# Working out the token places of two batches at the head of an attention's fourth round

## The reference

```python
logits = xf @ gate_w + gate_b
probs = jax.nn.softmax(logits, axis=1)
topk_p, topk_i = jax.lax.top_k(probs, TOP_K)
...
rank = jnp.cumsum(mask.astype(jnp.int32), axis=0)
slot = jnp.where(mask & (rank <= C), rank - 1, C)
...
xin = x_pad[idx]
h = jax.nn.relu(jnp.einsum('ecd,edh->ech', xin, w1) + b1[:, None, :])
out = jnp.einsum('ech,ehd->ecd', h, w2) + b2[:, None, :]
```

## Time and profile before

| | |
|---|---|
| Median of 3 runs | 1766.37 us (1758.09 to 1767.57) |
| The profiled execution | 1775.01 us, its span 1773.3 us |
| TensorE busy | 1382.5 us (78%) |
| VectorE busy | 1011.9 us (57%) |
| ScalarE busy | 690.0 us (39%) |
| GpSimd busy | 461.2 us (26%) |
| Mean granted TensorE clock | 0.868 of full speed |

### The profile page before, as it was taken

One profiled execution on the slowest core, in us unless ns is written; L12 is line 12 of the kernel. 1 busy time (PEld: TensorE's weight loads), 2 busy tenths in 40 slices (PEclk: granted clock), 3 DMA queues, 4 the chain that ended last, 5 costly groups with the idle time before them and its releaser, 6 DMA issues. The chain is left out here.

```text
span 1773.3 us, 26739 instructions
## 1 busy us (share of the span) xinstructions
PE 1382.5 (78%) x9650; PEld 837.1 (47%) x9650; DVE 1011.9 (57%) x2471; ACT 690.0 (39%) x1868; POOL 461.2 (26%) x577
## 2 busy tenths in 40 slices
PE   3677845858989948675886798989978967887998
PEld 2333423635555625353332456565655543344665
DVE  6554551154556643166454667676675864555886
ACT  3233431246656514242334455555542133333121
POOL 1000042244423342342000385858450001000000
PEclk8577867979999978787898799899898978988999
DMA  2443011150000010211000000000000010000000
GB/s 49 127 124 99 11 43 55 38 108 10 4 1 1 1 59 30 85 56 33 8 2 1 1 1 1 1 1 1 1 1 1 1 23 8 9 2 1 7 6 13
DMA packets 66999, 45.40 MB, mean 26 GB/s; under 512 B 17564, under 2 KB 60261, under 8 KB 66869
## 3 DMA queue, kind: packets, MB, share of 16 engines
q1 hardware_dynamic: 61013, 34.48, 7.3%
q0 software_dynamic: 4096, 8.40, 1.8%
q10 hardware_dynamic: 1760, 0.82, 0.2%
HBM read 24.91 MB, written 13.89 MB: 22 GB/s over the span
## 5 line engine op out<-in xcount | busy, mean ns | idle before, releaser
L3191 ACT ACTIVATE L2a_pr<-psum,L2a_negmax 128x512 f32<-128x512 f32 (+3 forms) x256 | 131.9, 526 | 131.8 <-DVE L2a_negmax L3261 73.3
L550 ACT ACTIVATE L1x_praw<-psum,L1x_negmax 128x154 f32<-128x154 f32 x256 | 96.2, 391 | 78.7 <-DVE L1x_negmax L642 78.5
L3059 PE MATMUL psum<-ident,L2a_pr 128*128 128x128 f32 x640 | 96.6, 301 | 34.1 <-DVE L2a_pT L3281 20.0
L312 POOL TENSOR_TENSOR L1x_pm<-L1x_praw,L1x_total 128x1024 f32<-128x1024 f32 x32 | 60.8, 1899 | 159.4 <-DVE L1x_total L648 102.4
L3059 PEld LDWEIGHTS psum<-ident,L2a_pr 128*128 128x128 f32 x640 | 81.1, 156 | 41.3 <-issue 25.1
L1519 DVE TENSOR_REDUCE L0x_negmax<-psum 128x6 f32<-128x924 f32 (+1 forms) x48 | 47.7, 1011 | 79.3 <-PE psum L1065 76.3
L1519 DVE TENSOR_REDUCE L3x_negmax<-psum 128x6 f32<-128x924 f32 (+1 forms) x48 | 47.8, 1011 | 69.2 <-PE psum L1065 58.1
L1519 DVE TENSOR_REDUCE L2x_negmax<-psum 128x6 f32<-128x924 f32 (+1 forms) x48 | 47.8, 1011 | 60.0 <-PE psum L1065 53.0
L642 DVE TENSOR_REDUCE L1x_negmax<-psum 128x4 f32<-128x616 f32 x64 | 50.8, 795 | 54.4 <-PE psum L364 50.6
L1957 DVE SCALAR_TENSOR_TENSOR L3f_acc<-psum,L3f_comb,L3f_acc 128x128 f32<-128x128 f32 x256 | 72.0, 343 | 8.4 <-PE psum L1861 5.0
L2950 POOL TENSOR_TENSOR L2a_pr<-L2a_pr,L2a_total 128x1024 f32<-128x1024 f32 x32 | 60.7, 1896 | 51.4 <-DVE L2a_total L3289 51.4
(11 more groups left out here) (695 smaller groups left out, 3548.3 us busy)
## 6 DMA issues: line engine op xcount, KB each, us to landing
expert_arena<-in_L_ffn_w SPq DMA_DIRECT2D x16, 256.0 KB, 4.9
group_in<-zero SPq DMA_DIRECT2D x2, 1472.0 KB, 11.2
L1f_xs<-group_in SPq DMA_DIRECT2D x10, 256.0 KB, 4.1
group_out<-L1f_ys SPq DMA_DIRECT2D x10, 256.0 KB, 2.6
...
```

What stands on the lines that cost most here:

```text
L312: nc.gpsimd.tensor_tensor(pm[:, n % 2].rearrange("p j t k -> p (j t) k"), praw[:, n % 3, :, :, 0:MAIN].rearrange("p j t k -> p (j t) k"), ...
L550: nc.scalar.activation(praw[:, n % 3, j, t, :], psum[:, 2 * u + j, x * CTX:(x + 1) * CTX], ACT.Exp, bias=negmax[:, n % 2, u, j, x:x + 1], ...
L3059: last = nc.tensor.transpose(psum[:, TURN + n // 4, n % 4 * P:(n % 4 + 1) * P], pr[:, m % RING, n * P:(n + 1) * P], core.ident[:])
L3191: ins = nc.scalar.activation(pr[:, i % RING, SEQ * j + lo:SEQ * j + hi], psum[:, bank + j, lo:hi], ACT.Exp, bias=negmax[:, i % RING, e:e + ...
```

## The change

In the fourth round (b = 3) the steps of group 0 move to its head: `rowsT` of both batches and `logits` ahead of the second chunk's scores, `best` ahead of `normalised(2)` on VectorE, `ranks` ahead of `output(2)`. Their variance root and `front` move into the third round. `HOSTED` goes from 5 to 6, which is 12 scatters in place of 10, and each pair after the first waits until the pairs before it have landed. `best` of group 1 moves from `sparse_experts` to the end of the attention; its one-hot choices get a tile of their own, `oh1`. In `sparse_experts` the `ranks` of group 1 go ahead of group 2's transposes.

```diff
@@ TensorE, round b
                     scoresT(b, 0)
+                    if dispatch and b == B - 1:
+                        pe.wait_ge(s["mx"], UNITS * B)
+                        pe.wait_ge(s["added"], B - 2)
+                        dispatch.rowsT(pe, 0, 0, xns[0], 1)
...
                     products(b - 1, NG)
+                    if dispatch and b == B - 1:
+                        pe.wait_ge(dispatch.s["xt"], 1)
+                        dispatch.rowsT(pe, 0, 1, xns[1], 1)
                     scores(f, 0, 1)
                     sums(b - 1, NG)
+                    if dispatch and b == B - 1:
+                        pe.wait_ge(s["mrow"], 2 * B)
+                        dispatch.logits(pe, 0, turned, 0)
...
-                    if dispatch and b == B - 1:
-                        pe.wait_ge(s["mrow"], 2 * B)
-                        dispatch.rowsT(pe, 0, 0, xns[0], 0)
...
                     if dispatch and b == B - 1:
-                        pe.wait_ge(s["added"], B - 2)
-                        dispatch.rowsT(pe, 0, 1, xns[1], 1)
+                        pe.wait_ge(dispatch.s["lg"], 1)
+                        dispatch.ranks(pe, 0, 0)
                     output(b - 1)
                     scoresT(b, 2)
-                    if dispatch and b == B - 1:
-                        dispatch.logits(pe, 0, turned, 0)
...
-                    if dispatch and b == B - 1:
-                        pe.wait_ge(dispatch.s["lg"], 1)
-                        dispatch.ranks(pe, 0, 0)
                     scoresT(b, 4)
@@ ScalarE, round b
                     exps(b, 0)
+                    if dispatch and b == B - 1:
+                        dispatch.rows_out(act, 0, turned[0], 1)
...
+                    if dispatch and b == B - 1:
+                        dispatch.rows_out(act, 1, turned[1], 1)
                     values(b - 1)
                     exps(b, 1)
-                    if dispatch and b == B - 1:
-                        for x in range(2):
-                            dispatch.rows_out(act, x, turned[x], x)
...
                     exps(b, 3)
+                    if dispatch and b == B - 2:
+                        dispatch.spread_root(act, 0)
                     if f < B:
                         max_rows(2 * f)
                     exps(b, 4)
...
-                    if dispatch and b == B - 2:
-                        dispatch.spread_root(act, 0)
@@ VectorE, round b
                     maxima(f, 0, 2)
-                    if dispatch and b == B - 1:
-                        dve.wait_ge(s["xt_ps"], B)
-                        dispatch.front(dve, v, 0, first_rows)
...
+                    if dispatch and b == B - 1:
+                        dispatch.logits_in(dve, 0, tmp["lg"], 0)
+                        dispatch.best(dve, v, 0, tmp["lg"], tmp)
                     normalised(b - 1)
+                    if dispatch and b == B - 1:
+                        dispatch.place(dve, v, 0, tmp, 0)
...
                     if dispatch and b == B - 1:
-                        dispatch.logits_in(dve, 0, tmp["lg"], 0)
-                        dispatch.best(dve, v, 0, tmp["lg"], tmp)
                         dispatch.front(dve, v, 1, dispatch.rows)
-                        dispatch.place(dve, v, 0, tmp, 0)
...
                     maxima(f, 6, 7)
+                    if dispatch and b == B - 2:
+                        dve.wait_ge(s["xt_ps"], B)
+                        dispatch.front(dve, v, 0, first_rows)
                     maxima(f, 7, 8)
...
                 kept(B - 1)
+                if dispatch:
+                    dispatch.best(dve, v, 1, dispatch.lg1[:], middle)
@@ Dispatch
-    HOSTED = 5
+    HOSTED = 6
@@ Dispatch.scatter
         for n in range(first + t0, first + t1):
+            if k == 0 and t0 == 0 and n:
+                pool.wait_ge(self.s["spread"], 16 * 2 * n)
             for r in range(2):
@@ sparse_experts, TensorE
+                dispatch.ranks(pe, 1, RANK)
                 dispatch.rowsT(pe, 2, 3, xn, 3)
                 dispatch.logits(pe, 2, [xnT], LOGITS)
-                dispatch.ranks(pe, 1, RANK)
@@ sparse_experts, VectorE
                 dispatch.front(dve, v, 2, xn)
-                dispatch.best(dve, v, 1, dispatch.lg1[:], tmp[1])
                 dispatch.place(dve, v, 1, tmp[1], RANK)
```

4 lines of the change are left out of this document (added).

## The result

The changed kernel takes 1779.32 us (median of 6, 1767.50 to 1784.32), the kernel before, run beside it, 1760.40 (6 runs, 1758.09 to 1767.57). The ratio of their runs is 1.0089, 95% interval 1.0062 to 1.0116: 15.7 us slower, with 10.9 to 20.4 in the interval (the medians lie 18.9 apart). The forecast was 1773 with 1763 to 1781, and "same" with 0.70. The time lies in the range. The change is slower by more than 0.5%, to which the forecast gave 0.27.

A forecast was written before the change was run, and what follows sets the result against it. GpSimd's chain of sixteen scatters before the read of slots_in was taken as the bound. Its first expert-stage scatter 9.1 + 3.6 = 12.7 us late, less 6.3 gained, gives +6.4: 1773 us from 1766.4, range 1763 to 1781.

The forecast's parts named there:

- P: First GpSimd scatter of the expert stage, after the barrier; forecast 12.7 us late, 9.1 without the lower clock.
- What the change gives behind the seam: Expert stage: the chain of sixteen scatters starts 5.2 us after P instead of 11.5, so 6.3 us sooner.
- Third round's end … Net +1.4: Moved root and its table load +1.5, eight row operations +1.2, exponential's table load saved −1.3: net +1.4 us.
- Fourth round's head: Transposes, logits and VectorE's choice come ahead of batch 2's normalising: its reciprocal at 223.3, 8.5 us late.
- Rival 4: Change is faster: VectorE has a gap for the choice and the output product isn't held; −3.5 us, 1763, chance 0.10.
- The clock in the fourth round, +3.6: TensorE's wait before batch 2's output product brings half clock for some 10 us; four slower groups, +3.6 us.
- Rival 1: TensorE's clock holds through the fourth round: +2.8 us, 1769, chance 0.22.
- rival 2: TensorE's clock stays low to the fourth round's end: +11 us, 1777, chance 0.20.
- From batch 3's reciprocal to P: 9.0 us to VectorE's drain, 3.4 for batch 2's choice, 1.76 from drain to first expert-stage scatter.
- GpSimd beside it: Paced hosted scatters, 4.3 us a pair (3.5 to 5.6): GpSimd's drain at 256.6, about together with VectorE's.
- rival 3: Paced scatters on GpSimd end last at the barrier, at 5.6 us a pair: +10 us, 1776, chance 0.06.
- Downstream only the start moves: Behind the read of slots_in everything shifts in start only; no term added to the sum.

The follow-up runs named there:

- choice_six: Kernel before with batch 2's choice at the attention's end, its rank products first in the expert stage, twelve unpaced hosted scatters: 1760.38 us, ratio 1.0016.
- before_again: The kernel before, unchanged, run once more for a second profile: 1760.61 us, ratio 1.0009.
- delay2: Kernel before plus four unused tiles cleared and a drain on GpSimd ahead of batch 3's scatters in the expert stage: 1780.76 us, ratio 1.0093 to the kernel before.
- fill3: Changed kernel plus eight needless identity products on TensorE ahead of the third round's scores that wait for the maxima: 1763.94 us, ratio 1.0026 to the kernel before.
- root_behind: Changed kernel with the variance root behind the third round's copy of the maxima instead of ahead: 1763.12 us, ratio 1.0013 to the kernel before.
- norm_first: Changed kernel with batch 2's normalising ahead of logits and choice on VectorE, ranks behind the second chunk's sums on TensorE: 1789.89 us, ratio 1.0050 to the kernel before.
- fill4: Changed kernel plus sixteen needless identity products on TensorE between the ranks and batch 2's output product: 1780.95 us, ratio 1.0085 to the kernel before.
- six_paced: Kernel before with batch 2's choice at the attention's end, its ranks first in the expert stage, twelve hosted scatters paced in pairs: 1770.11 us, ratio 1.0045.
- unpaced: Changed kernel without the waits between pairs of hosted scatters: 1797.85 us, ratio 1.0104 to the kernel before.

## Why the prediction was right or wrong

The range held partly by luck. The forecast added +6.4 us to 1766.4, the median of the three runs that it had; from 1760.4, the median of the six that were compared, the same sum gives 1767 and the same range ends at 1775, below the 1779.3 measured. The difference itself came out at 15.7 us where 6.4 were forecast, and by the forecast's own line of 0.5% the change is slower, where it had put 0.70 on no difference.

Counted from the mark, P is 87.1 − 70.3 = 16.8 us later, 4.1 more than forecast. By the forecast's own steps:

- *What the change gives behind the seam*: 6.3 us sooner after P. Measured 11.5 − 5.2 = 6.3 against the profile that the forecast read, and the same 5.2 behind P in choice_six, with nothing else of the change. The new kernel's side is right. But the 11.5 contains the 2.89 us wait, and in before_again and delay2 it is 9.7: against them the change gives 4.5.
- **"Third round's end … Net +1.4": the step that failed.** It measured +6.5 (39.45 − 32.94). The work itself is at most 2.0 (fill3). The other 4.5 is TensorE's clock, which I had weighed only for the fourth round's wait, though the sum itself gave TensorE a wait of 0.50 + 1.5 = 2.0 us here, beside a row in which a wait of 2.42 us had been enough. root_behind shows that the delay of the copy of the maxima decided it: with the 1.5 us of the root taken out of the term, its other two parts (+1.2 − 1.3) make −0.1, and −0.3 was measured.
- *Fourth round's head*: first exponential to reciprocal of batch 2 forecast as 223.3 − 212.7 = 10.6, measured 12.0; 10.8 in fill3. The same half clock, which lasts until 221.4, makes the rest. The head's mechanism and size were right. Rival 4 (VectorE has a gap, the output product isn't held) is refuted; in norm_first, where the output product isn't held, P is no sooner.
- *The clock in the fourth round, +3.6*: it fell as forecast, at 231.7 for 6.8 us, in place of 10; fill4 prices it at 1.9, and 1.7 at P. The sum from output product to batch 3's reciprocal, 16.2 without it, is 15.8 in fill4. Mechanism right, the term too large by half: from the output product on, groups of eight took 2.05, 2.09 and 1.66 us and the next 1.03 and 1.14: two and a half slow ones, not four. Rival 1 (the clock holds) and rival 2 (it stays low to the round's end) are both refuted: it was back at 1.00 from 238.5 to 252.2.
- *From batch 3's reciprocal to P*: forecast 9.0 + 3.4 + 1.8 = 14.2, measured 13.8. Right.
- *GpSimd beside it*: 3.75 us a pair where I took 4.3 of a range 3.5 to 5.6. The landing counts from the second scatter's issue, and the idle behind it is 1.5 us. VectorE ended last by 3.0, as forecast, so rival 3 didn't decide. In the old order of the round pacing is the bound: six_paced pays 6.2 for it. What no step of mine saw is that in the new order the stretch is 10 us longer without pacing (unpaced).

Together: +5.1 (third round) + 1.4 (head) − 2.0 (17.8 for 16.2 + 3.6, fourth round) − 0.4 = +4.1, as found. The read is then 10.4 us later than in the first profile, where 6.4 were forecast.

"Downstream only the start moves" holds for the code and not for the time. On the first chip the shift of the read is the change of the time: four kernels whose read moves by −2.8, +6.3, +10.9 and +18.3 us have, by their ratios, −2.5, +4.5, +8.9 and +18.5. These shifts are counted from the first profile of the kernel before, which has that chip's nameless wait and its long second attention.

On the others one must count from a profile without that wait. Up to the chain of sixteen delay2 is the kernel before; counted from there the chain, and the read 21.2 us behind it, is 12.4 us later in the changed kernel. Its time is +15.7 (10.9 to 20.4) and, once more, +13.9 (10.2 to 17.8): both intervals hold the 12.4. delay2 has +16.4 (11.1 to 21.8) for its 10.9. The other kernels there scatter to both sides: root_behind +2.3 for 3.6, fill3 +4.6 for 6.7, six_paced +7.9 for 4.3, fill4 +15.0 for 10.7, choice_six +2.8 for −1.8. Counted from before_again, where TensorE also kept its clock in the third round, the changed kernel's read is 14.9 later; but the seven other profiles on those two chips had the long stretch of half clock there. So 10 to 12 of the 16 us are shown to arise ahead of the read, and a kernel with a delay of 11 us there and nothing else is as slow. The remaining 3 to 5 us can't be told from the scatter of the time behind the read, and stay open.

So the largest error of the sum is one wait of 2 us that I had in my own numbers and didn't follow to the clock.
